# First layer's attention: the reciprocals of the softmax sums go through rows in memory instead of through TensorE

## The reference

```python
x_norm = _group_norm(x, gn_scale, gn_bias).reshape(b, seq, c)
qkv = x_norm @ w_qkv + b_qkv
q, k, v = (to_heads(q), to_heads(k), to_heads(v))
weight = jnp.einsum('bhld,bhsd->bhls', q * scale, k * scale)
weight = jax.nn.softmax(weight, axis=-1)
out = jnp.einsum('bhls,bhsd->bhld', weight, v)
out = out.transpose(0, 2, 1, 3).reshape(b, seq, c)
out = out @ w_out + b_out
return (x_flat + out).reshape(b, h, w, c)
```

## Time and profile before

| | us |
|---|---|
| median of 3 runs | 4119.28 |
| the runs | 4115.55 to 4120.51 |
| the profiled execution, its own time | 4118.52 |
| its span in the profile | 4116.5 |
| granted TensorE clock, mean share of full speed | 0.989 |

### The profile page before, as it was taken

One profiled execution on the slowest core, in us unless ns is written; L12 is line 12 of the kernel. 1 busy time (PEld: TensorE's weight loads), 2 busy tenths in 40 slices (PEclk: granted clock), 3 DMA queues, 4 the chain that ended last, 5 costly groups with the idle time before them and its releaser, 6 DMA issues. The chain is left out here.

```text
span 4116.5 us, 64395 instructions
## 1 busy us (share of the span) xinstructions
PE 3957.1 (96%) x22378; PEld 3310.1 (80%) x22378; DVE 2942.3 (71%) x5029; ACT 2552.0 (62%) x5577; POOL 1604.7 (39%) x1911
## 2 busy tenths in 40 slices
PE   8999999999999999999999889999999999999999
PEld 6888888888888878888888667777777777777777
DVE  3984974966948839849759656868686868686866
ACT  3874865856838838748658336565656555565656
POOL 1332432432433324324234223535454544454544
PEclk9999999999999999999999989999999999999999
DMA  2121121221221212211211402121212121222212
GB/s 85 42 70 44 42 72 41 59 66 31 53 62 37 62 46 46 66 44 42 79 35 42 147 1 62 62 62 62 62 62 62 62 59 65 54 71 47 75 44 62
DMA packets 113128, 235.51 MB, mean 57 GB/s; under 512 B 17260, under 2 KB 33704, under 8 KB 112808
## 3 DMA queue, kind: packets, MB, share of 16 engines
q1 hardware_dynamic: 112808, 231.41, 21.1%
HBM read 80.35 MB, written 33.55 MB: 28 GB/s over the span
## 5 line engine op out<-in xcount | busy, mean ns | idle before, releaser
L624 DVE TENSOR_REDUCE a_neg_max<-a_ps 128x1 f32<-128x1024 f32 x512 | 624.8, 1222 | 336.9 <-PE a_ps L447 336.9
L723 POOL TENSOR_TENSOR a_qk<-a_fold_s,a_fold_r 64x256 f32<-64x256 f32 x256 | 191.1, 746 | 1229.3 <-DVE a_fold_s L632 1229.3
L582 ACT ACTIVATE a_ph<-a_ps 128x512 fp32r<-128x512 f32 x1024 | 556.7, 593 | 172.7 <-PE a_ps L461 169.8
L641 DVE TENSOR_TENSOR a_pl<-a_ps,a_ph 128x512 fp32r<-128x512 f32 x1024 | 654.4, 679 | 8.9 <-ACT a_ph L582 5.6
L589 ACT ACTIVATE a_prob<-a_ps,a_neg_max 128x1024 f32<-128x1024 f32 x512 | 572.0, 1117 | 17.6 <-DVE a_neg_max L624 11.8
L461 PEld LDWEIGHTS a_ps<-a_ident,a_prob 128*128 128x128 f32 x4096 | 469.8, 140 | 112.7 <-issue 46.8
L461 PE MATMUL a_ps<-a_ident,a_prob 128*128 128x128 f32 x4096 | 540.7, 274 | 17.2 <-DVE a_pl L641 16.1
L482 PE MATMUL a_ps<-a_ph,a_v 128*128 128x256 f32 x2048 | 550.6, 302 | 0.0
L482 PE MATMUL a_ps<-a_pl,a_v 128*128 128x256 f32 x2048 | 509.1, 282 | 0.0
L1808 POOL TENSOR_SCALAR b_prob<-b_prob,b_row_inv 128x256 f32<-128x256 f32 x512 | 245.6, 480 | 562.2 <-DVE b_row_inv L1695 526.3
L446 PE MATMUL a_ps<-a_kh,a_qs 128*128 128x512 f32 x1024 | 408.4, 399 | 11.9 <-POOL a_kl L714 11.9
(11 more groups left out here) (258 smaller groups left out, 9456.6 us busy)
## 6 DMA issues: line engine op xcount, KB each, us to landing
a_qs<-a_qk SPq DMA_DIRECT2D x128, 256.0 KB, 3.7
a_kl<-a_qk SPq DMA_DIRECT2D x128, 256.0 KB, 4.6
a_xtok<-in_x SPq DMA_DIRECT2D x64, 256.0 KB, 4.8
b_xs<-x SPq DMA_DIRECT2D x64, 256.0 KB, 4.7
b_qs<-b_qh SPq DMA_DIRECT2D x64, 256.0 KB, 3.0
b_qs<-b_ql SPq DMA_DIRECT2D x64, 256.0 KB, 3.8
b_z<-x SPq DMA_DIRECT2D x64, 256.0 KB, 3.4
out<-b_ot SPq DMA_DIRECT2D x64, 256.0 KB, 2.0
```

The source lines that it names most:

```text
L582: act.activation(ph[:, b % 2, 4 * g:4 * g + 4, (u % 2) * P:(u % 2 + 1) * P], ps[:, 4 + n % 2, :].rearrange("p (k q) -> p k q", k=4), ACT.C ...
L624: dve.tensor_reduce(neg_max[:, i_:i_ + 1], ps[:, 2 * (i_ % 2):2 * (i_ % 2) + 2, :] .rearrange("p a b -> p (a b)"), AX, ALU.max, negate=Tru ...
L641: dve.tensor_tensor(pl[here], ps[:, 4 + n % 2, :].rearrange("p (k q) -> p k q", k=4), raw(ph[here]), ALU.subtract).then_inc(pl_ok, 1)
```

## The change

The two transposes of each pair on TensorE and ACT's copy into `fold_r` go away. Instead SP writes the two columns of `row_inv` of a pair to a row of 256 numbers in memory (`inverses_out`), and reads the row back, the same for 64 partitions, into `fold_r` (`inverses_in`), which now has four buffers. The read of pair b is issued behind the write of pair b+1. In the row the two units alternate (element 2q+n is query q of unit n), so the multiply reads `fold_r` in steps of two elements. SP's copies of queries and keys (`copies`), which stood in a loop of their own, are issued at fixed places between these, and the loads of the next image (`xtok`) are issued one for each of the last eight pairs. The waits on `inv_ok` and on the second copy fall away on TensorE; POOL waits for the row's arrival (`iv_ld`) and for the sum.

```diff
-        fold_r = R.take("a_fold_r", [P, 2, 256])
+        fold_r = R.take("a_fold_r", [P, ROWS, 256])
...
-            for h in range(NH):
+            def copies(h):
...
+            def inverses_out(b):
+
+                sp.wait_ge(inv_ok, at(inv_ok, b + 1))
+                sp.dma_start(inv_row[b].rearrange("(p n) -> p n", n=2), row_inv[:, 2 * b:2 * b + 2])\
+                  .then_inc(iv_st[b % 2], 16)
+
+            def inverses_in(b):
+
+                sp.wait_ge(iv_st[b % 2], at(iv_st[b % 2], 16 * (b // 2 + 1)))
+                if b >= ROWS:
+                    sp.wait_ge(att_ok, at(att_ok, b - ROWS + 1))
+                sp.dma_start(fold_r[own_half(b // NB), b % ROWS, :], inv_row[b].partition_broadcast(HD))\
+                  .then_inc(iv_ld[b % ROWS], 16)
+
+            copies(0)
+            copies(1)
+            for b in range(U // 2):
+                if (b + 1) % NB == 0 and (b + 1) // NB + 1 < NH:
+                    copies((b + 1) // NB + 1)
+                inverses_out(b)
+                if b >= 1:
+                    inverses_in(b - 1)
+                if more and b >= U // 2 - TT:
+                    t = b - (U // 2 - TT)
...
                     sp.dma_start(xtok[:, t, :], x[r + 1, t * P:(t + 1) * P, :]).then_inc(x_ld[t], 16)
+            inverses_in(U // 2 - 1)
...
-                    pe.wait_ge(inv_ok, at(inv_ok, b + 1))
...
-                        pe.wait_ge(fold_cp, at(fold_cp, 2 * b - 2))
-                    for n in range(2):
-                        u = 2 * b + n
-                        pe.transpose(ps[:, 6 + b % 2, 256 + n * P:256 + (n + 1) * P],
-                                     row_inv[:, u:u + 1].to_broadcast([P, P]), ident[:])
...
-                    if b >= 2:
-                        act.wait_ge(att_ok, at(att_ok, b - 1))
-                    act.activation(fold_r[own_half(h), b % 2, :], ps[own_half(h), 6 + b % 2, 256:512], ACT.Copy)\
                         .then_inc(fold_cp, 1)
...
-                pool.wait_ge(fold_cp, at(fold_cp, 2 * b + 2))
-                pool.tensor_tensor(qk[own_half(h), h // 2, (b % NB) * 256:(b % NB + 1) * 256],
-                                   fold_s[own_half(h), b % 2, :], fold_r[own_half(h), b % 2, :],
+                pool.wait_ge(iv_ld[b % ROWS], at(iv_ld[b % ROWS], 16 * (b // ROWS + 1)))
+                pool.tensor_tensor(qk[own_half(h), h // 2, (b % NB) * 256:(b % NB + 1) * 256]
+                                   .rearrange("p (n q) -> p n q", n=2),
+                                   fold_s[own_half(h), b % 2, :].rearrange("p (n q) -> p n q", n=2),
+                                   fold_r[own_half(h), b % ROWS, :].rearrange("p (q n) -> p n q", n=2),
                                    ALU.mult).then_inc(att_ok, 1)
```

More of the change, by code:

```diff
@@ L84, in layer0 @@
     QSCALE = 1.0 / HD
+    ROWS = 4
+    inv_row = nc.dram_tensor("a_inv_row", [U // 2, 256], F32, kind="Internal").ap()
     with ExitStack() as ctx:
@@ L161, in layer0 @@
         av_ps, fold_cp, fold_add, att_ok = sem("av_ps"), sem("fold_cp"), sem("fold_add"), sem("att_ok")
+        iv_st, iv_ld = [sem(f"iv_st{i}") for i in range(2)], [sem(f"iv_ld{i}") for i in range(ROWS)]
         ah_ok, al_ok, out_ps, res_ok, out_ok = sem("ah_ok"), sem("al_ok"), sem("out_ps"), sem("res_ok"), sem("out_ok")
@@ L164, in layer0 @@
                    xn_ok, xh_ok, xl_ok, pr_ps, qk_sb, vh_ok, vl_ok, staged, score, max_ok, exp_ok, tr_ps, ph_ok,
-                   pl_ok, inv_ok, av_ps, fold_cp, fold_add, att_ok, ah_ok, al_ok, out_ps, res_ok, out_ok]
+                   pl_ok, inv_ok, av_ps, fold_cp, fold_add, att_ok, *iv_st, *iv_ld, ah_ok, al_ok, out_ps, res_ok, out_ok]
         nums = [s.num for s in cleared]
@@ L366, in layer0 @@
         EACH.update({s_ld[0].num: 256, s_ld[1].num: 256, o_st.num: 16 * TT, pr_ps.num: len(groups), qk_sb.num: n_qk})
-        EACH.update({s.num: U for s in (score, max_ok, exp_ok, fold_cp)})
+        EACH.update({s.num: U for s in (score, max_ok, exp_ok)})
         EACH.update({s.num: 2 * U for s in (tr_ps, ph_ok, pl_ok)})
-        EACH.update({s.num: U // 2 for s in (inv_ok, av_ps, fold_add, att_ok)})
+        EACH.update({s.num: U // 2 for s in (inv_ok, av_ps, fold_cp, fold_add, att_ok)})
+        EACH.update({s.num: 16 * (U // 4) for s in iv_st})
+        EACH.update({s.num: 16 * (U // 2 // ROWS) for s in iv_ld})
         EACH.update({staged.num: STAGE * NH, ah_ok.num: len(SPLIT_AT), al_ok.num: len(SPLIT_AT)})
@@ L389, in sync_image @@
                     sp.dma_start(raw(kl[rows_, j, :]), qk[own_half(h), CT + p, :]).then_inc(s_ld[j], 16)
[L390 to L393, removed]
+            def inverses_out(b):
[18 more added lines that the diff above has]
+                    t = b - (U // 2 - TT)
+                    if t == 0:
+                        for j in range(2):
+                            sp.wait_ge(s_ld[j], at(s_ld[j], 64 * (NH // 2)))
                     sp.dma_start(xtok[:, t, :], x[r + 1, t * P:(t + 1) * P, :]).then_inc(x_ld[t], 16)
+            inverses_in(U // 2 - 1)
             sp.wait_ge(score, at(score, U))
@@ L494, in out_tile @@
                     pe.wait_ge(fold_add, at(fold_add, U // 2 + t - 3))
-                    pe.wait_ge(fold_cp, at(fold_cp, U + 2 * (t - 3)))
                 else:
@@ L569, in scalar_image @@
                         .then_inc(fold_cp, 1)
-                    if b >= 2:
-                        act.wait_ge(att_ok, at(att_ok, b - 1))
-                    act.activation(fold_r[own_half(h), b % 2, :], ps[own_half(h), 6 + b % 2, 256:512], ACT.Copy)\
-                        .then_inc(fold_cp, 1)
                 if 2 <= i_ < U + 2:
@@ L628, in vector_image @@
                     h = b // NB
-                    dve.wait_ge(fold_cp, at(fold_cp, 2 * b + 2))
+                    dve.wait_ge(fold_cp, at(fold_cp, b + 1))
                     if b >= 2:
```

## The result

The changed kernel takes 4209.47 us (median of 4 runs, 4204.74 to 4212.21), the kernel before 4117.9 us (4 runs, 4115.55 to 4120.51). The ratio is 1.0221, with a 95% interval of 1.0203 to 1.0239: 92 us slower. The prediction of 4123 us and its range up to 4143 us both missed.

A forecast was written before the change was run, and what follows sets the result against it. TensorE, busy for 96%, was taken to bound the kernel, with DVE close behind and POOL's chain at head changes. Per image -4.1 us of gains and +4.5 of losses made +0.4, for eight +3 to +4: 4123 us, range 4105 to 4143.

The forecast's parts named there:

- plain pairs: The 16 pair periods of an image without head change or extra DVE work: 5.50 us in even heads, 5.59 in odd.
- the whole gain: All transposes and copies removed, over the kernel: 4.1 us for an image, 33 us in all.
- The nine odd pairs: Plain pairs of odd heads, limited by DVE's `pl`: 0.14 us gained each, 1.3 us for an image.
- put at "none": Gain at the head changes and the 6 stretched pairs: none, since POOL's chain or DVE's extra work sets the pace.
- POOL's chain at the six head changes: Maximum, `fold_s`, multiply, line 714, scores: the added DMA makes it late, a loss of 4.5 us for an image.
- the later copies cost nothing of themselves: SP's copies of a head, issued some 3.5 us later: cost nothing, with some 1.5 us of cover left.
- T: Landing time of the row's read from its issue, ahead of POOL's multiply: taken as 2.1 us, range 1.8 to 2.5.
- the read lands late: Rival: read delayed behind the 128 eight-byte pieces or by slower memory; T from 2.2 us, 4142 us at 2.5; chance 0.36.
- The wait on the older write's arrival is long met: Before the read's issue on SP: that write was issued 5.7 us before, so the wait takes about 0.04 us.
- The next image's loads: nothing.: Loads issued one for each pair, the last some 8 us before its transposes: no cost.
- The formula: Whole kernel: net change = -33 + 48 x (T - 1.34) us.
- 24 x 0.76 + 24 x 1.02: Multiply's lateness at head changes: 0.76 us at pairs 4, 12, 20; 1.02 us at pairs 8, 16, 24, before cover.

The follow-up runs named there:

- no_row: Changed kernel without the row's DMAs and SP's new order; the multiply reads constant ones, so the division is left out: 4085.99 us, ratio 0.9927.
- early: Changed kernel, with POOL's line 714 (low half of the next head's keys) ahead of the multiply at head changes: 4069.99 us, ratio 0.9876.
- traffic: Kernel before, plus the same DMAs and SP's new order, into a spare tile for which only SP waits: 4116.73 us, ratio 0.9997.
- loads_apart: Changed kernel, with each of the next image's loads issued ahead of the pair's write instead of behind the read: 4193.51 us, ratio 1.0170.
- delay1: Kernel before, with one dummy POOL product ahead of line 714 at each head change, no row DMAs: 4142.61 us, ratio 1.0058.
- no_write: Changed kernel without the write and the wait on it; the read fetches a kilobyte of a weight: 4122.27 us, ratio 1.0016.
- swap: Changed kernel, with the read of pair b-1 issued ahead of the write of pair b, both behind b's reciprocals: 4162.51 us, ratio 1.0112.
- delay3: Kernel before, with three dummy POOL products ahead of line 714 at each head change, no row DMAs: 4248.16 us, ratio 1.0316.

## Why the prediction was wrong

**What was right.** TensorE sets the pace of plain pairs and DVE limits the gain: 5.50 and 5.59 us predicted, 5.51 and 5.63 measured; the whole gain 33 us predicted, 29.9 in `no_row`. That the sum came out so near is partly luck. The nine odd pairs gave 0.10 us each, not 0.14 (about 3 us less in all), and the head changes of pairs 8, 16 and 24, put at "none", gave 0.22 us each (5 us more). The place of the loss, POOL's chain at the six head changes, was right as well (`early`), and so was that the later copies cost nothing of themselves (`traffic`).

**The step that failed: T, "I take 2.1 us".** The read lands in 3.0 us at the median, 3.4 in the mean. The row of the same size was between tiles of SBUF, and I let it outweigh the rows from memory, which start at 2.5 us. The read alone takes 2.5 to 2.6. The other half us is the write ahead of it, which I had named as a cause and left to the rival "the read lands late". That rival is what happened, but I priced it only up to T = 2.5.

The issue of the write takes 0.33 us, not 0.46, which gives back a tenth. At the 48 head changes the multiply starts 3.44 us after the reciprocals at the median and 3.80 in the mean, against the 2.8 predicted.

**One T for all reads.** I took a landing as a number; it is a distribution with a long upper side, and a chain pays its mean. "The wait on the older write's arrival is long met" does hold: in the bad pair 12 the read's issue came 0.81 us after the write's, in pair 16 0.42, but the older write had landed 3.0 us earlier. Five reads were issued so late; what held them is open.

**"The next image's loads: nothing."** They cost nothing by their own lateness, but they delay the reads beside them: 8 us at pair 24, of the 16 that `loads_apart` gave.

**A linear price.** The formula charges 48 us for each us of T and has no term for the clock. Where the clock stays up this nearly holds, `delay1` included. Per head change of the changed kernel with its next pair, against `no_row`: in the 27 where the granted clock stayed at 1.00, the multiply was late by 1.35 us in the mean and the cost was 1.26. In the 21 where it fell to 0.50, the multiply was late by 2.39 us and the cost was 3.94. It fell once behind 18 of the waits, which cost 1.4 us more than the lateness, and stayed low for longer behind three (2.5 us more).

**The sum again.** The multiplies were late by 87 us in all (48 head changes, from `fold_s`), where I had 24 x 0.76 + 24 x 1.02 = 43. They cost 117 us in the pair periods: 87, plus 32 for the clock, less 2 that is covered. I had 36 after taking off 7 for cover. So of the 81 us that the prediction lacks, 44 are lateness, 32 the clock and 5 the cover. `no_row` took 24 us off the same pair periods, and 117 less 24 is the 93 us by which those of the changed kernel are longer than before. That is the whole of the measured 92; what is gained and lost outside them cancels to some 2 us.

With its right inputs, and short of the clock, the formula holds. It puts the multiply 0.7 + T after the reciprocals. In `no_write` it starts 2.83 us after them in the mean, as a T of 2.13 would have it (the 0.7 holds the issue of a write that this kernel does not have): -33 + 48 x (2.13 - 1.34) = +5 us; measured +6 against its kernel before. In the changed kernel the mean of 3.80 makes T 3.10 and the sum +51; most of the other 40 of the 92 us is the clock. That splits the error by its step: 3.10 - 2.10 is 48 us, and the linear price most of the rest.

## What to carry to other kernels

Before a DMA goes into a chain, look at what stands behind its consumer in the same engine's order: moving one independent instruction ahead of the consumer turned 92 us of loss into 48 us of gain, where a read that lands half a us sooner (`swap`) gave back only half of the loss, and one with no write in the queue at all (`no_write`) only came to zero. Price a landing by its mean and its tail in the traffic that it will have, including the write that goes ahead of it, and take rows with the same source, not only the same size. Price a wait of TensorE with the clock that it may cost after it, not by its length alone: here 1.4 to 1.6 us more for each time that it fell.

## What the runs showed of the hardware

- TensorE's clock fell to half after a single wait of 1.86 to 2.00 us in an otherwise busy stretch, in 34 of 48 cases (`delay3`), for about three us, and cost 1.6 us each time. In the changed kernel it fell behind 21 of 48 waits, the shortest of 1.78 us, and stayed at 1.00 behind the others, the longest of 3.08 us. In the same kernel and at the same place in the program it fell in some images and not in others.
- A write of 1 KB in 8-byte pieces lands in 3.2 us at the median (256 of them), later than 256 KB to memory (2.0), and loads of 256 KB issued behind such a write and a read take 5.4 us at the median, against 3.1 behind the read alone, and 2.7 where they are issued ahead of the write.
- 64 times the same kilobyte from memory lands in 3.0 us, 64 different kilobytes, of another tensor, in 4.1, behind the same write.
- Three POOL products of 0.6 us each, issued with no wait between them, hold the next up by 1.7 us.
